# Routed rows that add themselves onto memory: a mixture-of-experts output laid during attention

## What is computed

```python
x = L0_attn_in_features                                   # (4, 1024, 128)
x = x + attn(layernorm(x), w_q, w_k, w_v, w_o)            # causal
h = layernorm(x)
scores = softmax(h @ gate_w.T); top_scores, sel = top_k(scores, 2)
# for each of a token's 2 experts e, weighted by its score s:
#   y = s * ((silu(h @ w1[e]) * (h @ w3[e])) @ w2[e])
x = x + y_of_choice_0 + y_of_choice_1
```

## Time and profile before

| | us |
|---|---|
| three runs, median (lowest to highest) | 239.3 (238.39 to 239.92) |
| the profiled execution, device time | 239.59 |
| its span, first to last instruction | 237.8 |
| mean granted TensorE clock in it | 0.994 of full speed |

### The profile page before, as it was taken

One profiled execution on the slowest core, in us unless ns is written; L12 is line 12 of the kernel. 1 busy time (PEld: TensorE's weight loads), 2 busy tenths in 40 slices (PEclk: granted clock), 3 DMA queues, 4 the chain that ended last, 5 costly groups with the idle time before them and its releaser, 6 DMA issues.

```text
span 237.8 us, 6363 instructions
## 1 busy us (share of the span) xinstructions
PE 225.1 (95%) x1794; PEld 206.4 (87%) x1795; DVE 187.6 (79%) x851; ACT 145.8 (61%) x391; POOL 163.3 (69%) x204
## 2 busy tenths in 40 slices
PE   7989999999999999999999999999999999999960
PEld 6978888898799767877999998889999999999960
DVE  2479898879897789977898799957675656699994
ACT  2267787777877757855699665556575656566300
POOL 6523337788888888868577777777777777777700
PEclk9999999999999999999999999999999999999997
DMA  7999801111111111115124425534333333598368
GB/s 224 305 320 335 234 5 36 36 37 46 34 50 36 48 40 41 46 37 136 37 75 108 108 82 129 127 96 124 94 110 103 101 90 102 165 331 274 102 192 276
DMA packets 31978, 28.95 MB, mean 122 GB/s; under 512 B 4152, under 2 KB 26560, under 8 KB 31952
## 3 DMA queue, kind: packets, MB, share of 16 engines
q1 hardware_dynamic: 25216, 18.60, 28.5%
q0 software_dynamic: 4128, 8.59, 10.8%
q10 hardware_dynamic: 2608, 1.45, 2.0%
HBM read 16.34 MB, written 12.29 MB: 120 GB/s over the span
## 4 chain that ended last, share of the span: by engine, by line
PE 79%; POOL 6%; DMA 5%; DVE 3%; ACT 2%; issue 2%; ACTq 1%; POOLq 1%
PE scores L747 12%; PE turned L747 12%; PE scores L619 12%; PE weighed L680 11%; PE scores L768 6%; PE turned L645 5%; POOL expert_rows L524 4%; PE mixed L768 3%; PE weighed L768 3%; PE mixed L634 3%; PE mixed L633 3%; DMA choice_rows<-ysb,ycol 2%; DMA TL<-choice_rows 2%; DMA TL<-L_attn_w_o 2%; PE scores L764 2%
## 5 line engine op out<-in xcount | busy, mean ns | idle before, releaser
L535 POOL DMA_INDIRECT choice_rows<-ysb,ycol x65 | 65.0, 999 | 19.8 <-issue 14.6
L524 POOL DMA_INDIRECT expert_rows<-rows,slots x64 | 64.4, 1007 | 18.2 <-issue 13.2
L884 ACT ACTIVATE Wt<-W 128x512 f32 x71 | 44.1, 625 | 15.7 <-issue 15.7
L747 PE MATMUL scores<-xT,Wt 128*128 128x128 f32 x288 | 38.2, 276 | 0.8 <-issue 0.8
L619 PE MATMUL scores<-XX,TL 128*128 128x512 f32 (+3 forms) x96 | 38.1, 506 | 0.2 <-ACT TL L857 0.2
L680 PE MATMUL weighed<-TL,PT 128*128 128x136 f32 x272 | 37.0, 281 | 0.8 <-DVE X L1008 0.7
L747 PE MATMUL turned<-xT,Wt 128*128 128x128 f32 x280 | 37.1, 275 | 0.0
L747 PEld LDWEIGHTS scores<-xT,Wt 128*128 128x128 f32 x288 | 35.0, 192 | 1.1 <-issue 1.1
L680 PEld LDWEIGHTS weighed<-TL,PT 128*128 128x128 f32 x272 | 33.7, 190 | 1.7 <-issue 1.6
L747 PEld LDWEIGHTS turned<-xT,Wt 128*128 128x128 f32 x280 | 34.1, 192 | 0.0
L996 DVE TENSOR_REDUCE negmax<-scores 128x1 f32<-128x128 f32 (+7 forms) x32 | 23.5, 734 | 5.0 <-PE scores L619 5.0
(11 more groups left out here) (182 smaller groups left out, 456.1 us busy)
## 6 DMA issues: line engine op xcount, KB each, us to landing
xt<-expert_rows SPq DMA_DIRECT2D x71, 66.0 KB
TL<-choice_rows SPq DMA_DIRECT2D x15, 256.0 KB, 3.9
W<-L_ffn_w SPq DMA_DIRECT2D x2, 1024.0 KB, 9.7
out<-X ACTq DMA_DIRECT2D x9, 128.0 KB
choice_rows<-ysb,ycol POOLq DMA_INDIRECT x65, 2.3
X<-L_attn_in_features SPq DMA_DIRECT2D x2, 512.0 KB, 7.5
expert_rows<-rows,slots POOLq DMA_INDIRECT x64
out<-X SPq DMA_DIRECT2D x5, 128.0 KB
```

What stands on the lines that cost most here:

```text
L524: nc.gpsimd.indirect_dma_start(xs, bass.IndirectOffsetOnAxis(ap=slots[:, u, k:k + 1], axis=0), rows[:, u % ROWS_RING, k, :], None).then_in ...
L535: nc.gpsimd.indirect_dma_start(yb, bass.IndirectOffsetOnAxis(ap=ycol[:, q, 0:1].bitcast(u32), axis=0), ysb[:, q, :], None).then_inc(y_out[ ...
L747: mm(bank[2 + j % RING][:, c * P:(c + 1) * P], Wt[:, j % RING, c * P:(c + 1) * P], xT[:, j % RING, :], start=True, stop=True)
L884: copy(Wt[:, j % RING, :], W[:, ds(w * (SET // WIDE), SET)], ACT.Copy).then_inc(Wt_rdy, 1)
```

## The change

Before, a stored row replaced what was in memory, and VectorE added three things for each token: residual, choice 0, choice 1. Now the store adds its row onto what is there. SP lays the ground: in the region of choice 0 the residual of chunks 0 to 6 (copied from `X` as soon as attention has finished the chunk's tiles, 13 transfers of 128 or 256 KB), zeros for the last chunk; in the region of choice 1 and in the padding rows zeros (three transfers of 1 MB instead of one of 256 KB). Chunks 0 to 4 are laid before SP waits for the scattered rows, chunks 5 and 6 after the first eight loads. POOL waits for all of it before its first store. VectorE then makes one sum for a chunk, choice 0 plus choice 1, into `X`. Five chunks instead of three are summed between the gates, behind tiles 59, 61, 63, 65 and 67, and written by SP; the other two come after the last output tile and are written by ACT, whose loop runs from `N_SOON` to `N_LATER`. The last chunk is handled as before.

```diff
-N_SOON, ADD_AT = 3, [59, 61, 63]
+N_SOON, ADD_AT = 5, [59, 61, 63, 65, 67]
...
+        ZERO_ROWS = (E + SPARE) * P
+        ZERO_AT = range(N_TOK, YB_ROWS, ZERO_ROWS)
...
-            for k in range(K):
-                sp.dma_start(yv[:, k, LAST, :, :], padrows[:, 0:FIN, 0:D]).then_inc(y_zero, 16)
+            sp.dma_start(yv[:, 0, LAST, :, :], padrows[:, 0:FIN, 0:D]).then_inc(y_zero, 16)
+            for n in ZERO_AT:
+                sp.dma_start(yb[n:n + ZERO_ROWS, :].rearrange("(j p) d -> p j d", p=P),
+                             padrows[:, :, 0:D]).then_inc(y_zero, 16)
+
+            def lay_residual(c):
+
+                sp.wait_ge(x1_rdy, (c + 1) * FIN)
+                for n, z in pieces(c):
+                    i = 0 if n == CHUNKS[c][0] else 2
+                    sp.dma_start(yv[:, 0, c, i:i + z, :], X[:, n:n + z, 0:D]).then_inc(y_base, 16)
+
+            for c in range(HALF + 1):
+                lay_residual(c)
...
             load(0)
+            for c in range(HALF + 1, LAST):
+                lay_residual(c)
             with sp.Fori(1, M0 - 1) as m:
...
                 nc.gpsimd.indirect_dma_start(
                     yb, bass.IndirectOffsetOnAxis(ap=ycol[:, q, 0:1].bitcast(u32), axis=0),
-                    ysb[:, q, :], None).then_inc(y_out[q], 16)
+                    ysb[:, q, :], None, compute_op=ALU.add).then_inc(y_out[q], 16)
...
-                        pool.wait_ge(y_zero, 16 * K)
+                        pool.wait_ge(y_zero, 16 * (1 + len(ZERO_AT)))
+                        pool.wait_ge(y_base, 16 * sum(len(pieces(c)) for c in range(LAST)))
...
-            def add_choice(c, k):
+            def add_choices(c):
...
-                if k == 0:
-                    dve.wait_ge(yf_in[c], 16 * K)
-                else:
-                    dve.wait_ge(sum0, c + 1)
-                v.tensor_tensor(Xc, Xc, yf[:, c, k, :, :].rearrange("p (n t) d -> p n t d", t=2),
-                                ALU.add).then_inc([sum0, sum1][k], 1)
+                dve.wait_ge(yf_in[c], 16 * K)
+                y0, y1 = (yf[:, c, k, :, :].rearrange("p (n t) d -> p n t d", t=2) for k in range(K))
+                v.tensor_tensor(Xc, y0, y1, ALU.add).then_inc(sum1, 1)
...
-                for k in range(K):
-                    if t - k in ADD_AT:
-                        add_choice(ADD_AT.index(t - k), k)
+                if t in ADD_AT:
+                    add_choices(ADD_AT.index(t))
...
-            out_pair(*divmod(NT, OUT_LANES))
-            add_choice(N_SOON, 0)
-            out_pair(*divmod(NT + 1, OUT_LANES))
-            add_choice(N_SOON, 1)
-            out_pair(*divmod(NT + 2, OUT_LANES))
-            for c in range(N_SOON + 1, LAST):
-                for k in range(K):
-                    add_choice(c, k)
+            for t in range(NT, NT + LAG):
+                out_pair(*divmod(t, OUT_LANES))
+            for c in range(N_SOON, LAST):
+                add_choices(c)
```

## The result

The changed kernel takes 277.4 us (276.85 to 278.0, 4 runs), the kernel before 239.2 (238.39 to 239.92, 4 runs): a ratio of 1.158, 95% interval 1.153 to 1.162. The span of its profiled execution is 275.3 us instead of 237.8.

A forecast was written before the change was run, and what follows sets the result against it. POOL's chain of 64 stores, without slack, was taken to set the end. Moved work -0.8 us, landing +0.8 and store issue 64 x 0 left the span at 237.8 and the median at 239.3 us; range from 236.5 to 252.

The forecast's parts named there:

- term (1): Issue of an adding store on POOL: taken as 0 extra, upper end 0.48 us a store, x 64 = 30.7 us.
- Rival B: POOL's stores become dearer through generating a row's third address, with no slack to hide it: 245 to 252 us; chance 0.38.
- the ring: The 16 output buffers; with dearer stores they would hold TensorE, with many more than 10 waits of VectorE.
- The rule on read descriptors: Skill's rule: an adding transfer emits two read descriptors per chunk, at half a copy's rate, so POOL's 958 ns would grow.
- No slack on the store path: POOL's stores from 132 us on work off a backlog: a nanosecond more per store is 64 ns at the last one.
- The landing: Last adding store's landing, 4.85 us before: taken as +0.8 us, bounds 0 to 2.6 us.
- the moved work: VectorE's halved adds and early writes of chunks 3 and 4 in the tail: -0.8 us, ends 0 and -2.0.
- the fetch: Last fetch of routed rows in the tail, 4.30 us: could drop by some 0.9 us, half taken, 0.45.
- rival D: Faster: landing costs nothing extra, last store lands in 4.1 us, last fetch takes its quickest: 236.5 us; chance 0.10.
- VectorE's seven removed adds: Fourteen adds of 684 ns become seven, 4.8 us less on VectorE; claimed to bring nothing directly on the path.
- Laying residual and zeros: SP's early transfers during attention: issue priced at 45 us, 14 us of DMA time, costed at nothing.
- The list of signs: Expected profile: stores at 958 ns, last starting at 224 to 225; wrong by a dearer store above all, then disturbed attention.

The follow-up runs named there:

- e5: Changed kernel with adding stores of 64 rows instead of 128; 271.35 us beside 266.33 for the kernel before.
- e6: Kernel before with zeros laid everywhere and plain stores of 64 rows instead of 128; 266.49 us beside 266.33 for the kernel before.
- e17: Kernel before with a 128x64 fill on POOL ahead of each plain store; 241.07 us beside 239.20, ratio 1.0062.
- e18: Kernel before with a 128x640 fill on POOL ahead of each plain store; 271.95 us beside 239.20, ratio 1.137.
- e9: Changed kernel with only the stores of odd tiles adding, those of even tiles plain; 257.5 us beside 239.39 for the kernel before, ratio 1.074.
- e14: Kernel before with zeros laid in all result memory and adding stores, old order kept; 277.73 us beside 239.39, ratio 1.160.
- e15: Changed kernel with a 128x64 fill on POOL ahead of each adding store; 279.05 us, ratio 1.1636 to the kernel before.
- e13: The changed kernel itself, run again beside the kernel before at 239.39 us; 278.77 us, ratio 1.161.
- e16: Changed kernel with plain stores again, all else of the change kept; 238.34 us beside 239.2 for the kernel before, ratio 0.9972.
- e2: Kernel before with zeros laid in all result memory and adding stores, at the slower level; 282.0 us beside 266.75, ratio 1.0615.
- e19: Kernel before with plain stores and both choices added separately, but five chunks between the gates; 1.9 us slower, ratio 1.0078.
- e1: Changed kernel with plain stores again, all else kept, at the slower level; ratio 0.9986 to the kernel before at 266.75 us.

## Why the prediction was wrong, step by step

**The price of an adding store.** This is the step that failed. The term (1) of the sum, the issue on POOL, was put at nothing: "I take 0, by the nearest rows, because 16 bytes more a row left it unmoved". The rows compared a plain scatter with a plain store; they showed that bytes cost nothing (behind another DMA both are at 0.96 us; the scatters' median of 961 hides a second group at 1.03), and the operation was what changed. It measured 597 ns, above even the upper end of 479, which was half again on all 958 ns. e5 and e6 show why that bound wasn't one: it supposed that the price goes by addresses, but 415 of the 597 ns are fixed, and the part by rows rose from 0.95 to 2.4 ns, by more than half again too. An unseen operation of the engine that the chain hangs on has no upper bound in the rows of its plain form. Rival B, with 0.38 against the forecast's 0.44, named the place, and its arithmetic held: no slack from the start, 64 times the price, VectorE held by the ring in many more than 10 places (48). Its reason, a third address for each row, can account for the 182 ns that go by rows at most; for the 415 fixed ones there is no reason on record. Its size was too small, and with it the range, whose upper end of 252 reached a third of the way.

**The rule on read descriptors.** What the Trainium skill says, that an adding transfer reads two addresses per chunk (Collectives: The Full Stack, "The bandwidth ceiling"), speaks in the right direction. No run here splits the transfer into read descriptors; what the runs show is 144 packets for a store instead of 32 and a mostly fixed price on POOL. By that rule, taken as half again on 958 ns, the estimate would have been 270 us, nearer than mine and still 7 us short, since a rule on descriptors says nothing on a fixed part.

**No slack on the store path.** Held, and in both directions: 1.5 us for 0.026 us a store (e17), 32.8 for 0.51 (e18), 38 for 0.597, 18 for half of the stores (e9).

**The landing.** I took +0.8 us; the last landing went from 4.85 to 5.16, +0.3, in this trace, and to 5.40 (e14), 5.50 (e15) and 6.13 (e13) in others with adding stores, up to +1.3. So the term was right in size and within the bounds I gave (0 to 2.6). Its working was not: I took 0.2 us more of each DMA engine for a transfer, and the packets of POOL's queue took 21.7% of 275.3 us instead of 10.8% of 237.8, which is 0.5 us more for each store. The median landing of all stores went from 2.3 to 3.3 us.

**Output writes and adds.** I took -0.8 us for the moved work. e16 measured -0.7 (-0.1 to -1.2) where plain stores bound the end: right in size, and in part by luck, for the split was off in e16's trace: the fetch gave 0.1 instead of 0.45, and 1.2 came from the last store's landing, a gain that the forecast had left to rival D. In the changed kernel itself the fetch fell from 4.30 to 3.97 and the last write from 2.5 to 275.3 - 273.03 = 2.3, but e2, with the old order, has a fetch of 3.91 too, so that can't be put down to the moved work; beside e14 no gain could be told. VectorE's seven removed adds were worth nothing as such, as said; but e19 beside e16 shows that the single sum is what makes room for the early writes, which the forecast treated as free.

**Laying residual and zeros at nothing.** Held within what can be told: the first store starts at the same moment, e1 and e16 show no loss. A loss of some tenths of a microsecond at the start can't be excluded (first store at 132.7 in e16, 133.2 in e13). SP needed 7.71 us to issue the three zero transfers, where I had allowed 45.

**What it was to show.** The list of signs put the longer store first among what would make it wrong, and that is the line in which the two profiles differ.

## What to carry to other kernels

Before giving an instruction on the bounding engine another operation, find what that operation costs by itself: here 0.6 us of issue, unseen in any row of before, times 64. An engine that works off a backlog at constant intervals has no slack even where another engine is 95% busy; multiply the smallest change in its interval by the number of instructions left. Let an adding transfer go only where its queue waits anyway: at 2.0 us a tile the same edit cost 15 to 16 us instead of 38, and since the last adding store started 265.0 - 250.4 = 14.6 us behind the last plain one there (e2 and e1), it would by an estimate take tiles of 2.0 + 14.6 / 64 = 2.2 us to hide it.

## What the runs showed of the hardware

An adding indirect store of 128 rows of 512 bytes costs GpSimd 1555 ns to issue, beside 958 for a plain one; with 64 rows 1403 beside 897. It has 144 packets instead of 32 (80 instead of 32 with 64 rows). Its landing takes 3.3 us at the median instead of 2.3. The issue doesn't go by how busy the DMA engines are: in the changed kernel its median is 1555 ns in a stretch with the engines 53% busy and in one with 91%, where the landing takes 5.8 us. What the added 597 ns are spent on stays open.

One kernel can have two levels of time from job to job (239 and 267 us, each within 1.5% over 14 to 16 runs), with tiles at 1.44 or 2.0 us, on one and the same chip at different times; the cause is not known. An edit's cost changed by a factor of 2.5 between them (e2 and e14). A verdict from one level doesn't carry over unless one knows which engine's chain it hangs on.
